# Weighing the values of a cross-attention three key tiles at a time, from four weight buffers, in a chain of eight blocks

## The reference, cut to what matters

```
def _attn(q, k, v, mask):
    scores = einsum('bqhd,bkhd->bhqk', q, k) / sqrt(8)
    scores = where(mask, -inf, scores)
    w = softmax(scores, axis=-1)
    return einsum('bhqk,bkhd->bqhd', w, v)
```

## Time and profile before

| | us |
|---|---|
| three executions | 6654.61, 6659.54, 6660.70 |
| median | 6659.54 |
| profiled execution, first to last instruction (its span) | 6652.9 |
| median less that span | 6.6 |
| first score of slot 0 to last score of slot 95 | 200 to 3437 |

### The profile page before, as it was taken

The page is one execution under the profiler, slowest core; times in us unless marked ns, Lnnn a source line. Parts: engine busy times, 40 slices in busy tenths (PEclk is TensorE's granted clock), DMA queues, the critical chain, the costliest instruction groups (busy, mean ns, idle before and its releaser), DMA issues.

```text
span 6652.9 us, 141291 instructions
## 1 busy us (share of the span) xinstructions
PE 6159.3 (93%) x56229; PEld 4429.8 (67%) x56229; DVE 3930.9 (59%) x8713; ACT 3325.9 (50%) x6401; POOL 2242.2 (34%) x2179
## 2 busy tenths in 40 slices
PE   6899899999999989999989999999789999989998
PEld 4566566665666656666653877777567777756983
DVE  3777777777777777777765334444544444444553
ACT  1565656656566565665654334444333333333763
POOL 4554555555555555555520000000011111136440
PEclk6899999999999999999989889999789999998998
DMA  1665656656666565665740010000000000021000
GB/s 56 105 111 83 99 94 99 106 91 103 93 98 111 85 100 100 96 108 87 110 95 5 13 38 29 29 33 24 26 15 15 10 15 12 13 81 36 2 1 23
DMA packets 396488, 407.90 MB, mean 61 GB/s; under 512 B 125575, under 2 KB 372946, under 8 KB 393786
## 3 DMA queue, kind: packets, MB, share of 16 engines
q1 hardware_dynamic: 395834, 398.85, 33.8%
HBM read 158.00 MB, written 0.46 MB: 24 GB/s over the span
## 4 chain that ended last, share of the span: by engine, by line
PE 69%; DVE 8%; POOL 7%; issue 6%; ACT 4%; DMA 2%; SPq 1%; POOLq 1%; DVEq 0%; ACTq 0%
PE psum L2214 10%; PE psum L2181 9%; PE psum L1551 6%; PE psum L1539 6%; PE psum L1525 6%; PE psum L2226 4%; PE psum L1565 4%; PE psum L1573 3%; PE psum L1671 3%; POOL slot_context L3399 2%; PE psum L434 2%; DVE row_max L1890 2%; PE psum L420 2%; PE psum L1680 1%; DMA key_stack<-key_parts 1%
## 5 line engine op out<-in xcount | busy, mean ns | idle before, releaser
L1890 DVE TENSOR_REDUCE row_max<-psum 112x1 f32<-112x500 f32 x2304 | 1443.7, 669 | 285.3 <-PE psum L1539 280.3
L2011 ACT ACTIVATE weights<-psum 125x448 f32<-125x448 f32 x2304 | 1155.4, 544 | 769.3 <-PE psum L1525 754.3
L1525 PEld LDWEIGHTS psum<-query_stack,key_stack 121*125 121x125 bf16 x9216 | 830.4, 140 | 368.4 <-issue 165.5
L1539 PE MATMUL psum<-key_stack,query_stack 97*112 97x500 bf16 x2304 | 907.8, 395 | 102.1 <-DVE row_max L1890 78.9
L1525 PE MATMUL psum<-query_stack,key_stack 121*125 121x112 bf16 x9216 | 932.3, 224 | 70.1 <-ACT weights L2011 65.0
L2767 POOL TENSOR_TENSOR l_ctx_v<-l_ctx_v,l_ctx_w 125x512 f32<-125x512 f32 x48 | 61.1, 1272 | 2223.1 <-DVE l_ctx_v L2761 2223.1
L2294 DVE TENSOR_REDUCE l_stat<-psum 128x1 f32<-128x1500 f32 (+1 forms) x224 | 391.6, 1748 | 576.6 <-PE psum L2181 576.6
L2214 PE MATMUL psum<-l_ctx_v,l_turned 125*128 125x128 f32 x5376 | 713.6, 281 | 16.0 <-ACT l_turned L2252 12.3
L2214 PEld LDWEIGHTS psum<-l_ctx_v,l_turned 125*128 125x128 f32 x5376 | 643.0, 191 | 58.5 <-ACT l_turned L2252 39.9
L1551 PE MATMUL psum<-weights,values 125*17 125x112 f32 x18432 | 678.0, 266 | 0.2 <-ACT weights L2011 0.2
L1551 PEld LDWEIGHTS psum<-weights,values 125*17 125x17 f32 x18432 | 379.4, 97 | 263.6 <-ACT weights L2011 144.7
(11 more groups left out here) (527 smaller groups left out, 10264.3 us busy)
## 6 DMA issues: line engine op xcount, KB each, us to landing
key_stack<-key_parts SPq DMA_DIRECT2D x1728, 125.0 KB, 4.5
ctx_t<-in_ctxT SPq DMA_DIRECT2D x96, 750.0 KB
l_ctx_v<-in_ctxV SPq DMA_DIRECT2D x32, 750.0 KB
query_stack<-query_parts SPq DMA_DIRECT2D x576, 28.0 KB, 3.7
l_ctx_t<-in_ctxT SPq DMA_DIRECT2D x16, 750.0 KB
slot_context<-in_ctxV SPq DMA_DIRECT2D x16, 750.0 KB
key_stack<-ctx_mask_rows SPq DMA_DIRECT2D x576, 3.9 KB
sm_w<-in_sm_w SPq DMA_DIRECT2D x3, 2048.0 KB
```

Source lines behind the costliest of these rows:

```text
L1525: mm = e.matmul(self.k.psum[0:KN, h, (p % 4) * QC:(p % 4 + 1) * QC], ks[:, p, kt * KN:(kt + 1) * KN], q[:, p * QC:(p + 1) * QC])
L1539: e.matmul(self.k.psum[0:QC, 2 + n % 2, 0:500], q[0:ROWS_MAX, p * QC:(p + 1) * QC], ks[0:ROWS_MAX, p, c * 500:(c + 1) * 500]).then_inc(sel ...
L1890: e.tensor_reduce(self.largest[:, i % PAIRS, i // PAIRS:i // PAIRS + 1], k.psum[0:QC, 2 + i % 2, 0:500], AX.X, ALU.max, negate=True).then_ ...
L2011: e.activation(half(self.p[kt % 2], h), self.k.psum[0:KN, h, 0:HALF], ACT.Exp).then_inc(self.exped.sem, 1)
```

## The change

The number of weight buffers goes from two to `RING` = 4. The PE no longer calls `weigh_tensor` in every step. In steps 3, 6 and 9 it weighs the three tiles before (0 to 2, 3 to 5, 6 to 8) in a row, and in step 0 of the next slot tiles 9 to 11. ACT waits, before the exponentials of a tile, for the weighing of the tile four before it. The number of instructions, their shapes and what each engine computes stay as they are; only the PE's order and the index of the buffer change. The place within the step (after the scores and maxima, ahead of the fixed and the phase work) stays too.

```diff
+BATCH, RING = 3, 4
...
-            self.p = [sb(f"weights{i}", [KN, T])[:, :] for i in range(2)]
+            self.p = [sb(f"weights{i}", [KN, T])[:, :] for i in range(RING)]
...
-        w, v = self.p[kt % 2], self.v[s % 3]
+        w, v = self.p[kt % RING], self.v[s % 3]
...
-                if 0 <= s < NS and kt > 0:
-                    self.weigh_tensor(e, s, kt - 1)
-                if 1 <= s <= NS and kt == 0:
-                    self.weigh_tensor(e, s - 1, KT - 1)
+                if kt % BATCH == 0:
+                    at, first = (s, kt - BATCH) if kt else (s - 1, KT - BATCH)
+                    if 0 <= at < NS:
+                        for t in range(first, first + BATCH):
+                            self.weigh_tensor(e, at, t)
...
-                    if h == 0 and s * KT + kt >= 2:
-                        e.wait_ge(self.weighed.sem, self.weighed(s, kt) - 2)
-                    e.activation(half(self.p[kt % 2], h), self.k.psum[0:KN, h, 0:HALF], ACT.Exp).then_inc(
+                    if h == 0 and s * KT + kt >= RING:
+                        e.wait_ge(self.weighed.sem, self.weighed(s, kt) - RING)
+                    e.activation(half(self.p[kt % RING], h), self.k.psum[0:KN, h, 0:HALF], ACT.Exp).then_inc(
                         self.exped.sem, 1)
```

## The result

The changed kernel takes **6720.0 us** (median of 4 runs, 6715.7 to 6724.7) against 6660.1 us: a ratio of 1.0087, 95% interval 1.0072 to 1.0101. Slower, as forecast, by 60 us instead of 84. The sum came out nearly right; the terms in it did not, as the profile shows at once.

A forecast was written before the change was run, and what follows sets the result against it. The PE bounds the kernel, with DVE second. Per phase 3 x 1.4 + 3 x 0.6 + 2.0 - 1.0 = 7.0 us, over 12 phases +84 us, gives 6744 us; range 6655 to 6825, the forecast alone 6690 to 6805.

The forecast's parts named there:

- The bound and the mechanism of the thin steps: PE sets the pace; without weighing it waits for DVE's row maxima: steps 4 to 6 +0.59 us, 1 to 3 +0.60.
- the 70 I had given as a sign: Sign of being right: PE waits for row maxima in block 0 up from 74.6 us by some 70 or more.
- One tile's weighing takes 0.51: PE cost of weighing one tile, 0.51 us start to start, taken as unchanged for weighings in a row.
- 0.09 more where float32 work follows: PE cost of a step's scores and maxima: 0.88 us, plus 0.09 us when float32 work comes next.
- The clock: Rival, much slower: new waits of about 1 us lower the granted clock in slots 0, 6, 7; 6805 us, chance 0.07.
- the second of the prediction's signs against itself: Sign of being wrong: a granted clock below 0.97 over the slots.
- Slots 3 to 5 at 0.6 us: Self-attention there is a filler of its own, so each slot gets only 0.6 us longer, bounds 0 and 1.4.
- the held slots: Slots 1, 2 and 5, where ACT or POOL hold the PE: four weighings leave such waits, +2.0 us a phase.
- Step 9's gain: Step 9 of the phase: three weighings made while ACT changes tables for the square root, -1.0 us a phase.
- The buffers at nothing: The ring of four weight buffers never holds ACT, so it costs nothing.
- ACT's copy of the sums covered: Step 0: ACT's copy waits 1.02 us longer, covered by the 0.94 us key matmul; uncovered up to 1 us a slot.
- The rival "faster": Gathered weighing saves switches between float32 and bf16, 43 to 115 us, without waits for DVE: 6581 us, chance 0.11.

The follow-up runs named there:

- experiment 2: Changed kernel with two tiles weighed in a row at every even step instead of three at every third; 6747.3 us, ratio 1.0129.
- experiment 3: Kernel before with four buffers and weighing runs in thin steps: three tiles in step 3, two in 5, 7, 9, 11, one in 0; 6519.3 us.
- experiment 4: Changed kernel plus twelve small bf16 matmuls before the PE's wait for POOL's query block, self-attentions 0 and 2 of each phase; 6676.7 us.
- experiment 1: Kernel before, still one tile weighed in each step, with four weight buffers instead of two; 6660.7 us, ratio 1.0001.
- experiment 6: Kernel before with four buffers and two tiles weighed in a row in steps 3, 5, 7, 9, 11 and 0; 6516.5 us, ratio 0.9784.

## Why the prediction was right, and where it wasn't

- **Direction and size**: 6744 forecast, 6720 measured, inside 6655 to 6825 and inside the forecast's own 6690 to 6805. It was right partly by luck, because two errors cancelled: a saving of some 160 us or more that it had at nothing, and the clock and waits that it had too small.
- **The bound and the mechanism of the thin steps** held. The PE waits for its bank in step 6 (1.19 us against 1.33), for ACT in step 8 (0.25 against 0.40), and runs at even steps lose 87 us with waits for row maxima 102 us up (experiment 2). But in the changed kernel these waits rose by 36 us (76.7 to 113.0, both lines; by 15 in the line that I had named), not by the 70 I had given as a sign, with 26 us more on the row maxima's parts at L1604, which I had put down as a gain. Those for exponentials rose by 23, within the 15 to 40 named. A slot 7 grew by 0.4 us and not by 1.4.
- **"One tile's weighing takes 0.51", three 1.53**, was the step that failed. It measured 1.275. With it, "0.09 more where float32 work follows" was wrong as a rule: the gap comes before a weighing, and keys behind a maximum start after 0.215 and take 0.84. The prediction had listed weighings in a row at clearly less than 0.51 us as a sign against itself, and that sign appeared. By the medians a run less saves 0.125 + 0.092, and keys or values not behind a weighing 0.10 more: the change has 8 starts fewer and 4 such exits a slot, 2.1 us, or 205 us over 96 slots. From the totals (58 us longer, 147 more waiting, half of 139 more at 0.50) the saving comes out at 147 + 70 - 58 = 159 us; waits too short to be recorded fit between the two, which I haven't separated. For the pairs at even steps the same sum leaves 59 us (145 more waiting, half of 22 more at 0.50, less 97), where the medians give 125, so that account is a rough one where waits are many. Where they are few it closes better: for the order of experiment 3 it gives 183 us (29 more waiting, half of 31, and 138 shorter) and the medians 173 (six starts and five exits fewer).
- **The clock** had a chance of 0.07, and was placed in slots 0, 6 and 7. It fell in slots 2 and 3 instead (57 and 78 us more at 0.50, the first partly scatter), in good part behind waits for POOL, and costs about 70 us by the added time at 0.50 (an estimate, half of 139), of which experiment 4 gave 43 back. The granted clock of 0.95 over the slots was the second of the prediction's signs against itself that appeared. The Trainium skill (TensorE: Matmul & The Clock Gate, section A second HAM failure mode: psum-queue depth-cycling) describes short idle times between groups of matmuls that make the clock swing. The trace agrees: many short waits, none above 2.9 us, and more time at the lower level. But the hand-over waited for at steps 35 and 44 was not that of a PSUM bank; it was that of POOL's query block.
- **Slots 3 to 5 at 0.6 us** measured +3.7, -0.4 and -0.6 us a slot; **the held slots**: the sum had 2.0 us a phase for them. The waits of slots 1, 2 and 5 rose by 54 us, 4.5 a phase, and two new ones, at steps 35 and 44, were not among the terms. The wait at 35 is 1.03 us, but the low clock behind it cost more: filling it gave 25.5 us over eleven phases, 2.3 each. **Step 9's gain** didn't come: in slot 0 it lasts 3.13 us, before 2.74 (medians).
- **The buffers at nothing** and **ACT's copy of the sums covered** held: experiment 1 is at 1.0001, and the PE waits for the copy once, for 0.5 us.
- **The rival "faster"** priced a gain of the right kind, starts saved, at 43 to 115 us; it is there, and larger. What decided against it was the place of the runs. Move them to the odd steps and it wins (experiments 3 and 6).

## What to carry to other kernels

When an in-order engine feeds others through two buffers each, as here, try its own filler work in the steps that are short, not in those that are long: the same six runs a slot were worth +87 us at even steps and -144 us at odd ones. Price a run of like instructions from a run if the trace has one, since three weighings cost 1.275 us and not 3 x 0.508. Look past the wait that an edit creates to the granted clock behind it: 139 us more at 0.50, at half their length, are more than this change's whole loss of 60 us. And check for each place that the filler meets the wait: only one of its two places did here.

## What the runs showed of the hardware

- Eight float32 weighing matmuls with 17 stationary columns (16 in the trace) cost 0.508 us alone, 0.891 in a run of two, 1.275 in a run of three; the distance ahead of a run is 0.092 us longer than ahead of another bf16 group (0.307 against 0.215), and the float32 key matmuls behind one take 0.94 instead of 0.84 us. It isn't the change of type as such, since keys straight behind bf16 lose nothing. What it is remains open.
- Waits of the PE of 1.03 us at step 35, in stretches that had others, were followed by 3.4 to 6.8 us at half clock in eleven phases of eleven; those of 1.42 us at step 44 in five. With 0.77 us of small matmuls in front of the first, none of the eleven was left. At step 44, unfilled, there were then ten. Waits of 0.2 and 0.4 us at the same places (experiment 3) had none behind them.
- A row maximum's matmul that waits for its bank starts 0.145 to 0.147 us after DVE's read has ended (all 41 and 54 waits that the profiles of the changed kernel and of experiment 2 put down to a DMA).
